# Deformable sampling in a vision tower: row differences with clamped ramps, the differences on GpSimd, and the second batch norm's constants taken from VectorE and ScalarE

## The reference, cut to what matters

```python
h = conv2d(x, stem_w, stem_b, 4)                  # 16 x 96 x 24 x 24
h = leaky_relu(batchnorm(h, bn1_g, bn1_b, bn1_m, bn1_v))
offset = conv2d(h, off_w, off_b, 4)               # 16 taps x (y, x) for each of 36 tokens
h = deform_conv(h, offset, dcn_w, dcn_b)
h = leaky_relu(batchnorm(h, bn2_g, bn2_b, bn2_m, bn2_v))

def deform_conv(x, offset, w, b):
    py = base_y + kh + off[:, :, 0]
    px = base_x + kw + off[:, :, 1]
    # v00, v01, v10, v11: x at the four pixels around (py, px), zero outside the image
    sampled = v00*(1-wy)*(1-wx) + v01*(1-wy)*wx + v10*wy*(1-wx) + v11*wy*wx
    return einsum('bckhw,ock->bohw', sampled, w) + b
```

## Time and profile before

| | |
|---|---|
| time, median of 3 runs | 466.15 us (461.22 to 468.23) |
| the profiled execution, its own time | 466.46 us |
| its span in the trace | 464.7 us |
| between span and time | 1.76 us |
| mean granted TensorE clock | 0.967 of full speed |
| stem, until the first transpose of the sampling | 0 to 31.5 us |
| sampling, until the last samples are taken out | 31.5 to 145.9 us |
| the rest (convolution, attention, experts) | 145.9 to 464.7 us |

### The profile page before, as it was taken

One profiled execution on the slowest core, in us unless ns is written; L12 is line 12 of the kernel. 1 busy time (PEld: TensorE's weight loads), 2 busy tenths in 40 slices (PEclk: granted clock), 3 DMA queues, 4 the chain that ended last, 5 costly groups with the idle time before them and its releaser, 6 DMA issues. The chain is left out here.

```text
span 464.7 us, 8988 instructions
## 1 busy us (share of the span) xinstructions
PE 409.4 (88%) x3083; PEld 331.3 (71%) x3083; DVE 321.0 (69%) x704; ACT 249.6 (54%) x652; POOL 141.8 (31%) x140
## 2 busy tenths in 40 slices
PE   8976769889878789899888898888999999999997
PEld 4234446556556778787667776665999999999986
DVE  2575779898882574446884467964688887797763
ACT  3674778688861225775553375651664266246320
POOL 1004362454442432235552134832230220221000
PEclk9989989899999999999999999976999999999999
DMA  8360524343301800300000300000512322231001
GB/s 182 75 176 13 133 67 108 82 114 95 102 12 30 298 2 29 101 3 1 2 2 1 118 2 2 1 3 1 179 60 69 121 59 103 74 118 51 0 0 40
DMA packets 12124, 30.57 MB, mean 66 GB/s; under 512 B 3628, under 2 KB 6220, under 8 KB 11960
## 3 DMA queue, kind: packets, MB, share of 16 engines
q1 hardware_dynamic: 11848, 30.06, 22.4%
q10 hardware_dynamic: 240, 0.04, 0.0%
HBM read 28.70 MB, written 0.52 MB: 63 GB/s over the span
## 5 line engine op out<-in xcount | busy, mean ns | idle before, releaser
L535 PE MATMUL ps<-weights,hT 120*96 120x288 f32 (+1 forms) x320 | 86.5, 422 | 19.7 <-POOL weights L236 17.4
L535 PEld LDWEIGHTS ps<-weights,hT 120*96 120x96 f32 (+1 forms) x320 | 51.5, 168 | 48.7 <-POOL weights L236 21.8
L236 POOL TENSOR_TENSOR weights<-dist_y,hat_x 120x576 f32<-120x576 f32 x16 | 52.9, 3306 | 83.9 <-DVE dist_y L336 57.4
L1384 PE MATMUL ps<-w,hid_hi 128*128 128x384 f32 (+1 forms) x240 | 67.9, 355 | 1.1 <-DVE rest L1468 1.0
L441 ACT ACTIVATE dist_y<-pos,row_shift 120x576 f32<-120x576 f32 x80 | 56.7, 770 | 15.6 <-POOL weights L236 15.6
L1411 ACT ACTIVATE hidden<-ps 128x576 f32<-128x576 f32 x48 | 31.1, 648 | 56.9 <-PE ps L1303 54.5
L1385 PE MATMUL ps<-w,hid_lo 128*128 128x192 f32 (+1 forms) x240 | 60.1, 250 | 0.0
L1081 ACT ACTIVATE a_probs<-ps,a_minus_peak 108x108 f32<-108x108 f32 (+1 forms) x144 | 47.3, 341 | 20.0 <-DVE a_minus_peak L1133 20.0
L1455 DVE TENSOR_TENSOR hid_lo<-hidden,hid_hi 128x576 fp32r<-128x576 f32 x48 | 46.0, 993 | 16.5 <-ACT hid_hi L1415 16.5
L1303 PE MATMUL ps<-x_hi,w_hi 128*128 128x288 f32 x192 | 56.2, 305 | 0.9 <-PEq L947 0.9
L1303 PE MATMUL ps<-x_lo,w_hi 128*128 128x288 f32 x192 | 55.0, 301 | 0.0
(11 more groups left out here) (155 smaller groups left out, 780.7 us busy)
## 6 DMA issues: line engine op xcount, KB each, us to landing
pos<-pos_dram SPq DMA_DIRECT2D x16, 540.0 KB, 4.4
raw<-in_w SPq DMA_DIRECT2D x8, 768.0 KB, 4.3
raw<-in_w SPq DMA_DIRECT2D x8, 576.0 KB, 3.8
patches<-in_patches SPq DMA_DIRECT2D x6, 216.0 KB, 5.4
dcn_w<-in_dcn_w SPq DMA_DIRECT2D x1, 1152.0 KB, 8.9
samples<-extra SPq DMA_DIRECT2D x12, 64.0 KB, 2.1
a_raw<-in_a_wq SPq DMA_DIRECT2D x1, 768.0 KB, 5.0
a_raw<-in_a_wk SPq DMA_DIRECT2D x1, 768.0 KB, 6.4
```

The lines of the kernel that those rows point to most:

```text
L236: eng.tensor_tensor(weights[0:r, t, :], dist_y[0:r, t, :], hat_x[0:r, s, :], ALU.mult).then_inc(ready, 1)
L535: ins = nc.tensor.matmul(ps[0:C1, 2 * (b % 2) + a, 0:HALF], hT[0:r, b % 2, t, :], weights[0:r, t, a * HALF:(a + 1) * HALF], start=(t == 0) ...
L1384: nc.tensor.matmul(ps[0:n, 4 + t % 4, 0:2 * DIM], hid_hi[:, s, f, t0:t0 + n], w2[s][:, f, :, :].rearrange("p a d -> p (a d)"), start=(f == ...
```

## The change

The weight along y becomes a ramp in place of a tent. With 25 differences of neighbouring rows, h[k-1] - h[k] with a row of zeros above and below the image, the sample is the sum over k of clamp(py - k + 1, 0, 1) times that difference, up to a sign that the sign of `hat_x` cancels. 25 x 24 values are exactly 5 full tiles of 120.

- ScalarE's |y| becomes Relu with a shifted bias, and only for tiles 0 to 3; the ramp of tile 4 is VectorE's `ramp` (add the bias, max with 0).
- `falls` is gone; `product` is one scalar_tensor_tensor, min(dist_y, 1) x hat_x, and VectorE does all five tiles.
- `h_act` has 24 zeros at each end (PAD = 624), set by GpSimd; the differences of 96 x 600 go into `h_step`, a ring of DRING = 4. That of image 0 is made by VectorE after the stem's last leaky ReLU, those of images 1 to 15 by GpSimd (`row_steps`), which starts once all 16 leaky ReLUs are done, and from image 4 on waits for the transpose of the image four before. TensorE transposes `h_step`; transpose_h(b) waits for it.
- ScalarE copies `hT` in one instruction in place of two.
- The second batch norm's constants are worked out by GpSimd on 96 partitions x 2 values early in the stem (`dcn_norm`), stored to DRAM and loaded again as `dcn_norm` on 128 partitions. SyncE has both DMAs, each with its wait, between the load of `dcn_w` and `store_positions(1)`.

```diff
-NT = -(-SIDE // ROWS)
-LAST = PIX - (NT - 1) * TILE
+STEPS = SIDE + 1
+NT = STEPS // ROWS
+PAD = SIDE * (SIDE + 2)
+DIFFS = SIDE * STEPS
+DRING = 4
...
                     if b >= PRING:
-                        sp.wait_ge(dist_y_ready, NT * (b - PRING + 1))
+                        sp.wait_ge(dist_y_ready, (NT - 1) * (b - PRING + 1))
+                        sp.wait_ge(ramp_ready, b - PRING + 1)
...
+                sp.wait_ge(norm_ready, 1)
+                sp.dma_start(P["norm_dram"].rearrange("a (p k) -> p a k", k=DC), dcn_norm_at[:, :, :]).then_inc(norm_stored, 16)
+                sp.wait_ge(norm_stored, 16)
+                sp.dma_start(P["dcn_norm"][:, :, :].rearrange("p a d -> p (a d)"), P["norm_dram"].rearrange("(o a) d -> o (a d)", o=1).to_broadcast((128, 2 * DIM))).then_inc(P["dcn_normed"], 16)
...
+                nc.gpsimd.memset(h_act[:, :, 0:SIDE], 0.0).then_inc(edges_set, 1)
+                nc.gpsimd.memset(h_act[:, :, PAD - SIDE:PAD], 0.0).then_inc(edges_set, 1)
...
-                product(nc.gpsimd, pool, 0, 0, POOL_T, pool_weights, waits=False)
-                product(nc.gpsimd, pool, 1, 1, POOL_T, pool_weights)
-                with nc.gpsimd.Fori(1, B // 2) as pair:
-                    for s in range(2):
-                        product(nc.gpsimd, pool, pair * 2 + s, s, POOL_T, pool_weights)
+
+                def row_steps(b):
+
+                    if b >= DRING:
+                        pool.wait_ge(hT_ready, b - DRING + 1)
+                    nc.gpsimd.tensor_tensor(h_step[:, b % DRING, :], h_act[:, b, 0:DIFFS], h_act[:, b, SIDE:PAD], ALU.subtract).then_inc(step_ready, 1)
+
+                def dcn_norm():
+
+                    steps = Steps(pool, dcn_step)
+                    pool.wait_ge(par_loaded, 16)
+                    steps.done(nc.gpsimd.tensor_scalar(dcn_var[:, :], dcn_par[:, :, 3], EPS, None, ALU.add))
+                    steps.done(nc.gpsimd.tensor_tensor(dcn_norm_at[:, 1, :], dcn_par[:, :, 4], dcn_par[:, :, 2], ALU.subtract))
+                    steps.wait()
+                    steps.done(nc.gpsimd.tensor_tensor(dcn_var[:, :], dcn_var[:, :], P["minus_half"][0:C1, 0:1].to_broadcast((C1, DC)), ALU.pow))
+                    steps.wait()
+                    steps.done(nc.gpsimd.tensor_tensor(dcn_norm_at[:, 0, :], dcn_var[:, :], dcn_par[:, :, 0], ALU.mult))
+                    steps.wait()
+                    steps.done(nc.gpsimd.tensor_tensor(dcn_norm_at[:, 1, :], dcn_norm_at[:, 1, :], dcn_norm_at[:, 0, :], ALU.mult))
+                    steps.wait()
+                    nc.gpsimd.tensor_tensor(dcn_norm_at[:, 1, :], dcn_norm_at[:, 1, :], dcn_par[:, :, 1], ALU.add).then_inc(norm_ready, 1)
+
+                pool.wait_ge(edges_set, 2)
+                dcn_norm()
+                pool.wait_ge(h_done, B)
+                for b in range(1, B):
+                    row_steps(b)
...
-                def falls(b, t):
-
-                    r = pixel_rows(t)
-                    dve.wait_ge(dist_y_ready, b * NT + (t + 1))
-                    nc.vector.tensor_scalar(dist_y[0:r, t, :], dist_y[0:r, t, :], 1.0, 0.0, ALU.subtract, ALU.min).then_inc(fall_ready, 1)
-
-                def hats(b, s, waits=True):
+                def ramp(b, s, loads, waits=True):
+
+                    if waits:
+                        dve.wait_ge(weights_ready, b * NT)
+                    dve.wait_ge(pos_loaded[s], loads * 16)
+                    nc.vector.tensor_scalar(dist_y[:, DVE_T, :], pos[:, s, 0, :], P["row_shift"][0:TILE, DVE_T:DVE_T + 1], 0.0, ALU.add, ALU.max).then_inc(ramp_ready, 1)
+
+                def hats(b, s):
 
                     dve.wait_ge(dist_x_ready, b + 1)
+                    nc.vector.tensor_scalar(hat_x[:, s, :], dist_x[:, s, :], 1.0, 0.0, ALU.subtract, ALU.min).then_inc(hat_x_ready, 1)
+
+                def product(b, s, t, waits=True):
+
+                    if t == 0:
+                        dve.wait_ge(hat_x_ready, b + 1)
+                    if t == DVE_T:
+                        dve.wait_ge(ramp_ready, b + 1)
+                    else:
+                        dve.wait_ge(dist_y_ready, b * (NT - 1) + (t + 1))
                     if waits:
-                        dve.wait_ge(pool_weights, b - 1)
-                    nc.vector.tensor_scalar(hat_x[:, s, :], dist_x[:, s, :], 1.0, 0.0, ALU.subtract, ALU.min).then_inc(hat_x_ready, 1)
-
-                def image_weights(b, s, first=False, last=False):
+
+                        if t == NT - 1:
+                            dve.wait_ge(samples_ready, b)
+                        else:
+                            dve.wait_ge(weights_used, b * (NT - 1) + (t + 1 - (NT - 1)))
+                    nc.vector.scalar_tensor_tensor(weights[:, t, :], dist_y[:, t, :], 1.0, hat_x[:, s, :], ALU.min, ALU.mult).then_inc(weights_ready, 1)
+
+                def image_weights(b, s, loads, first=False, last=False):
 
                     for t in range(NT):
-                        if t < NT - 1:
-                            falls(b, t + 1)
-                        elif not last:
-                            hats(b + 1, 1 - s, waits=not first)
-                            falls(b + 1, 0)
-                        if t != POOL_T:
-                            product(nc.vector, dve, b, s, t, weights_ready, waits=not first)
+                        if t == NT - 1 and not last:
+                            hats(b + 1, 1 - s)
+                        product(b, s, t, waits=not first)
+                        if t == 0:
+                            ramp(b, s, loads, waits=not first)
...
-                    if b == 3 * QUAD - 1:
-
-                        dve.wait_ge(par_loaded, 16)
-                        nc.vector.tensor_scalar(dcn_var[:, :], dcn_par[:, 3, :], EPS, None, ALU.add).then_inc(var_ready, 1)
...
+                dve.wait_ge(edges_set, 2)
+                dve.wait_ge(h_done, 1)
+                nc.vector.tensor_tensor(h_step[:, 0, :], h_act[:, 0, 0:DIFFS], h_act[:, 0, SIDE:PAD], ALU.subtract).then_inc(first_step_ready, 1)
...
-                    nc.scalar.activation(hT[:, s, 0:NT - 1, :].rearrange("p t c -> p (t c)"), ps[0:TILE, 4 + s, 0:(NT - 1) * C1], ACT.Copy).then_inc(hT_copied, 1)
-                    nc.scalar.activation(hT[0:LAST, s, NT - 1, :], ps[0:LAST, 4 + s, (NT - 1) * C1:NT * C1], ACT.Copy).then_inc(hT_copied, 1)
+                    nc.scalar.activation(hT[:, s, :, :].rearrange("p t c -> p (t c)"), ps[0:TILE, 4 + s, 0:NT * C1], ACT.Copy).then_inc(hT_copied, 1)
...
-                        wait_made(act, b - 1, t)
-                    nc.scalar.activation(dist_y[:, t, :], pos[:, s, 0, :], ACT.Abs, bias=P["row_shift"][0:TILE, t:t + 1]).then_inc(dist_y_ready, 1)
+                        act.wait_ge(weights_ready, (b - 1) * NT + (t + 1))
+                    nc.scalar.activation(dist_y[:, t, :], pos[:, s, 0, :], ACT.Relu, bias=P["row_shift"][0:TILE, t:t + 1]).then_inc(dist_y_ready, 1)
...
-                        pe.wait_ge(h_done, B)
+                        pe.wait_ge(first_step_ready, 1)
+                    else:
+                        pe.wait_ge(step_ready, b)
...
-    row_shift[:, 0:NT] = -(p[:, None] // SIDE + ROWS * np.arange(NT))
+    row_shift[:, 0:NT] = 1 - (p[:, None] // SIDE + ROWS * np.arange(NT))
```

112 lines of the change are left out of this document (37 added, 75 removed).

## The result

The changed kernel takes 448.78 us (median of 4 runs, 447.85 to 450.1) against 466.6 for the kernel before (4 runs, 461.22 to 468.23): ratio 0.9645, 95% interval 0.9596 to 0.9695. 17.8 us were gained where 21 were forecast. The profiled execution took 448.42, its span 446.6 (464.7 before), so the two profiles differ by 18.1.

A forecast was written before the change was run, and what follows sets the result against it. The prediction took the VectorE-GpSimd handover to bound the sampling. Start 4.6 us and steady part 18.5 make 23.1 less (19.0 at 5.56 an image); taking 21, 466.46 - 21 = 445.5 us, range 442 to 457.

The forecast's parts named there:

- the steady part: Sampling from image 2 on: 5.27 us an image in place of 6.59, TensorE's pace, 18.5 us less over 14 images.
- A: Sampling's steady part: each difference also waits for VectorE's operation under way and costs VectorE such a loss; 451.6 us, chance 0.18.
- B: Sampling: differences get turns only when VectorE runs out, TensorE waits every other image, mean 6.5 us; 460.6 us, 0.12 with D.
- C: Sampling: every image starved once the head start is used up, 470 us, or 491 with TensorE's clock falling; chance 0.08.
- D: VectorE's new product takes 0.95 us in place of 0.75, so turns sum as before; 461.9 us, 0.12 with B.
- SyncE's wait for the stored norm: On SyncE ahead of store_positions(1) to (3): could last until 31 us, costing nothing as no store is needed before 39.8.
- The start: From the stem's end to image 2's first sampling matmul: sample(2) at 49.0 and not 53.58, 4.6 us gained.
- 1.17 + 0.2: First transposes: 1.17 us gained, lost with 0.2 more if GpSimd's first difference wins the turn there.
- some 10: GpSimd's differences left for the 14 images from image 2 on, the others made earlier in VectorE's idle stretches.
- The norm's constants: Stem's end: table load and Sqrt leave ScalarE, ten small operations leave VectorE; first transposes at 30.36, 1.17 us earlier.
- 2 us for turns not packed: Sum of terms: 21 us taken in place of 23.1, since turns of VectorE and GpSimd are not packed without gaps.

The follow-up runs named there:

- unsharing alone: The kernel before with tile 2's product moved from GpSimd to VectorE, no ramps or differences: 451.73 us, ratio 0.9706.
- the doubled differences: The changed kernel with GpSimd making each difference of images 7 to 15 twice: 458.29 us, ratio 0.9881.
- The held version: The changed kernel with GpSimd's differences after image 1's held until VectorE has made image 0's five products: 444.13 us, ratio 0.9559.
- VectorE's version: The changed kernel with all 16 differences on VectorE, a ring of two, GpSimd idle in the sampling: 441.56 us, ratio 0.9496.
- the last run: The paced kernel with its waits moved, meant to put the differences of images 2 and 3 in a gap of VectorE: 446.52 us, ratio 0.9556.
- the order of positions alone: The changed kernel with only the load of image 2's positions moved ahead of the last store of positions: 444.51 us, ratio 0.9591.
- paced: The changed kernel with image 2's positions loaded ahead of the last store and GpSimd's differences released one an image: 444.35 us, ratio 0.9575.
- the old norm on the best version: All differences on VectorE and image 2's positions loaded early (438.35 us), with the norm's constants made as in the kernel before: 443.77 us, ratio 0.9558.

## Why the prediction was right, and where it wasn't

**The bound and the steady part: right.** The handover bounded the sampling (unsharing alone gives 2.9 of 3.6 per cent, with the old arithmetic), and the forecast of TensorE's 5.27 an image holds to the digit. A, B and C were about this part, and none came about as a time: a difference costs VectorE 1.24 us without A's losses (and with one more of them an image the sum of turns does bound), the differences that wait for a turn are hidden by the ring (B, C), and a product without a turn takes 0.75 (D). SyncE's wait for the stored norm lasted until 32.68 (31 forecast), and as forecast it held up nothing.

**The start: wrong by 6.6 us in the profile, by 3.0 where the clock was kinder** (51.97, the doubled differences). The step that failed is "VectorE has idle stretches while place_offsets(3) and then the positions of image 2 are on their way, which is room for the differences of images 3, 4 and 5". The order gave no reason for them to wait for such a stretch: they were ready at 29.6, when GpSimd was free, and ran beside image 0's first products. I priced the first of them winning one turn (1.17 + 0.2) and not five in a row. The held version shows the rest of this chain to be sized right (34.29, 40.02, 45.52), and VectorE's version the end of it (48.31 for 49.0). The number of differences left for the steady part came out too: 9 fell behind the start of sample(2), for "some 10".

**The clock: a rival's term in the wrong place.** The low clock was weighed only for a late ring (C). It came in the start: 2.28 us idle, then 16 matmuls in 6.65, 2.6 us that had no term in the sum, and 1.0 more on sample(2) (20 matmuls in 6.04). Whether filling such a stretch helps was not shown.

**The norm's constants: the term held, and I misread it later.** The 1.17 us were the first transposes at 30.36 in place of 31.53, net of image 0's new difference, and they came at 30.38. What they are not is the worth of taking the constants off VectorE, as two expectations took them. That is 2.7 us where nothing disturbs, because the last two small operations, which nobody waited for in the kernel before, would now stand ahead of the difference. In the changed kernel it is nothing measurable (448.78 against 449.14), since the burst swallows as much.

**The sum.** Steady part 18.5 forecast; from sample(2) to the end of the sampling 18.2 measured. Start 4.6 forecast, 2.0 lost. That is 23.1 forecast by the terms and 16.1 measured. Two things that have nothing to do with the start hid most of the 7: I had taken off 2 us for turns not packed, which the steady part did not need, and 2.0 came back in the profiles with a better clock at the experts. So 445.5 missed 448.78 by only 3.3, and that it was so near is luck.

## What to carry to other kernels

When work is moved to an engine that takes turns with another, ask when it is *released*, not only how much there is of it: a ring with room and an input that is ready make a burst at the worst moment. Here the whole of it was cheaper on the engine that had been relieved (0.78 us a difference, against 1.24 lost to each turn): 7.2 us better by the medians, and 10.4 with one load put ahead of a store. And measure the plain undoing first: unsharing the old kernel gave some five sixths of the gain with no new arithmetic. Before two profiles are compared, look at the clock row by row: here the same instructions gave starts 3.6 us apart.

## What the runs showed of the hardware that I had not expected

- Between VectorE and GpSimd two patterns occur. Five differences in a row that began before VectorE's operations alternated with them (hat 1.04, product 1.92, ramp 1.71). One released while VectorE's operations were running without a gap got no turn until they stopped (3.4 us in the last run, 12.1 in that of the order of positions alone), and then took 1.31 to 1.36. A pause of VectorE of 0.21 us was enough to let it in. In the steady part, though, differences got their turn ahead of a hat or a ramp with no pause to be seen. What decides, the runs don't settle.
- The low clock comes behind TensorE's idle stretches, but neither at a fixed place nor each time. In the changed kernel it lay behind the 2.28 us stop (16 matmuls in 6.65); with the same instructions, in the run of the doubled differences, it lay ahead of the stop and the 12 matmuls behind it took 3.15. Behind the 1.91 us ahead of the first transposes these took 1.03 in the changed kernel and 0.60 in others. After stops of 2.27, 3.70 and 5.83 us other kernels had it (16 in 5.81, 20 in 7.28 and in 6.17), and the version with all differences on VectorE, with two stops of 1.91, had a granted clock of 1.00 from 30 to 60 us.
- The work behind the sampling is the same in all these kernels, and took from 313.6 us (paced) to 318.7 (the old norm on the best version), along with the clock at the start of the experts. Differences under that are better read from the start of the token convolution than from a total, as far as the clock ahead of it was the same.
